# Causal masks moved from TensorE to VectorE and GpSimd in a decoder's self-attention, with the value products directly behind the shifts

## What is computed

```python
q = (x @ wq.T + bq).reshape(B, S, 16, 64).transpose(0, 2, 1, 3)     # likewise k and v
q, k = rope(q, k)
scores = einsum('bhqd,bhkd->bhqk', q, k)
scores = where(triu(ones((S, S)), k=1), -inf, scores)                # the causal mask
attn = softmax(scores / 8, axis=-1)
out = einsum('bhqk,bhkd->bhqd', attn, v)
x = layernorm(x + out @ wo.T + bo)
```

## Time and profile before

| | us |
|---|---|
| median of 3 runs | 2767.6 |
| lowest and highest | 2765.4 and 2783.56 |
| the profiled execution, its own time | 2774.03 |
| its span, first to last instruction | 2772.2 |
| mean granted TensorE clock | 0.896 |

### The profile page before, as it was taken

How to read it: one execution, slowest core, us unless ns; L and a number is a source line. 1 busy time by engine, 2 the same in 40 slices (tenths; PEclk the granted TensorE clock), 3 DMA queues, 4 the chain that set the end, 5 groups by cost and what they waited for, 6 DMA issues and landing times. The chain is left out here.

```text
span 2772.2 us, 46887 instructions
## 1 busy us (share of the span) xinstructions
PE 2118.1 (76%) x18469; PEld 1188.9 (43%) x18469; DVE 1536.0 (55%) x2539; ACT 1026.4 (37%) x1420; POOL 1026.9 (37%) x658
## 2 busy tenths in 40 slices
PE   6888888888888888888888886378586686783565
PEld 3434434434434444444444343256455464562222
DVE  4553553553644554544545531357767677677778
ACT  1322222232322222222222222058186293591555
POOL 0344344344434443443434444306326145053003
PEclk7999999999999999999999998699899798996685
DMA  6111111111112112112111100100000000001001
GB/s 185 24 29 41 28 44 41 28 29 41 28 37 49 28 22 48 28 22 47 26 25 35 30 20 5 52 6 3 6 2 2 6 3 2 7 3 33 0 0 61
DMA packets 51198, 78.02 MB, mean 28 GB/s; under 512 B 26144, under 2 KB 38560, under 8 KB 46112
## 3 DMA queue, kind: packets, MB, share of 16 engines
q1 hardware_dynamic: 41760, 74.71, 10.7%
q10 hardware_dynamic: 9216, 0.27, 0.2%
HBM read 36.68 MB, written 4.19 MB: 15 GB/s over the span
## 5 line engine op out<-in xcount | busy, mean ns | idle before, releaser
L639 POOL TENSOR_TENSOR acc<-acc,probs 128x1024 f32<-128x1024 f32 (+3 forms) x320 | 558.4, 1745 | 500.6 <-ACT probs L468 257.8
L468 ACT ACTIVATE probs<-psum 128x1024 f32<-128x1024 f32 (+3 forms) x384 | 292.2, 809 | 589.5 <-PE psum L364 335.4
L276 PE MATMUL psum<-xT,wqk 128*128 128x512 f32 x512 | 301.7, 746 | 94.7 <-ACT probs L468 52.0
L553 DVE TENSOR_REDUCE maxa<-psum 128x2 f32<-128x1024 f32 (+3 forms) x256 | 256.7, 1021 | 203.8 <-PE psum L327 139.3
L951 ACT ACTIVATE onehot<-psum 128x1024 bf16<-128x1024 f32 x320 | 323.0, 1038 | 14.9 <-DVE ctx L1101 8.3
L532 DVE TENSOR_TENSOR turned<-raw,rot 128x512 f32<-128x512 f32 x128 | 115.8, 905 | 379.9 <-ACT raw L451 350.8
L1246 POOL TENSOR_TENSOR vs<-vs,wgt 128x1280 f32 x64 | 151.7, 2371 | 444.7 <-DVE wgt L1093 444.7
L350 PE MATMUL psum<-operands 64*128 64x512 f32 (+3 forms) x1536 | 308.1, 517 | 10.1 <-ACT probs L468 5.1
L378 PE MATMUL psum<-probs,vals 128*64 128x512 f32 (+3 forms) x1536 | 290.1, 499 | 0.0
L850 PEld LDWEIGHTS psum<-piece,onehot 128*128 128x128 bf16 x7680 | 259.1, 99 | 71.5 <-ACT vs L955 14.2
L850 PE MATMUL psum<-piece,onehot 128*128 128x64 bf16 x7680 | 267.2, 194 | 9.2 <-ACT onehot L951 5.7
(11 more groups left out here) (194 smaller groups left out, 3003.0 us busy)
## 6 DMA issues: line engine op xcount, KB each, us to landing
operands<-turned SPq DMA_DIRECT2D x128, 256.0 KB, 4.1
wqk<-in_wqk SPq DMA_DIRECT2D x16, 512.0 KB, 3.0
xT<-in_xT SPq DMA_DIRECT2D x4, 1024.0 KB, 6.9
wv<-in_wv SPq DMA_DIRECT2D x16, 256.0 KB, 2.5
y<-in_x SPq DMA_DIRECT2D x1, 4096.0 KB, 21.7
wo<-in_wo SPq DMA_DIRECT2D x16, 256.0 KB, 2.6
out<-res SPq DMA_DIRECT2D x16, 256.0 KB, 2.1
bv<-in_bv SPq DMA_DIRECT2D x16, 128.0 KB, 3.2
```

Source lines behind the costliest of these rows:

```text
L276: last = nc.tensor.matmul(dst[:, eo, :], wqk[:, kt, c:c + P], x[:, kt, hf * BANK:(hf + 1) * BANK], start=kt == 0, stop=kt == KT - 1)
L468: nc.scalar.activation(probs[u % PBUF][:, :, 0:width], slot("s", n, u)[:, :, 0:width], ACT.Exp, scale=1.0 / D ** 0.5).then_inc(s_exp, 1)
L553: V.reduce_max(dst, slot("max", n, c)[:, :, 0:width], AX.X).then_inc(s_mread, 1)
L639: G.tensor_tensor(dst, dst, src, ALU.add).then_inc(s_acc, 1)
```

## The change

- `mask_q`, `mask_k`, `halves` and their matmuls go. A new fp32 tile `later` (0, and -1e30 above the diagonal) is loaded; three DMAs of constants become one.
- `maximum` on VectorE: for each of the 8 masked chunks one `tensor_tensor` adds `later` to the last 128 columns of both heads, in PSUM, then a wait for it, then the reduction.
- `add_probs` on GpSimd: for each of the 8 diagonal units one `affine_select` zeroes the probabilities above the diagonal in the first 128 columns of both heads in `probs`, counted by the new semaphore `s_tri`, then a wait for it, then the copy or addition.
- `weigh` on TensorE waits for `s_tri` where the unit is diagonal.
- `weigh` of units 2m-2 and 2m-1 stands directly behind the shifts of step m, ahead of the chunks and the full work. At m = 0 it stays where it was.

```diff
+DIAGONAL = [u for u, (kt, hf) in enumerate(UNITS_S) if kt * P >= hf * BANK]
+MASKED = [c for c, (qt, hf) in enumerate(CHUNKS) if (qt + 1) * P <= (hf + 1) * BANK]
...
-        halves = sb("halves", [P, 2, P], BF16)
-        mask_q = sb("mask_q", [P, 2, P], BF16)
-        mask_k = sb("mask_k", [P, 2, P], BF16)
+        later = sb("later", [P, P])
...
@@ max_chunk
                 for hh, rows in enumerate(HEADS):
                     last = nc.tensor.matmul(dst[:, hh, 0:width], ops[p][rows, 0, qt * P:(qt + 1) * P],
-                                            ops[p][rows, 1, hf * BANK:hf * BANK + width],
-                                            start=True, stop=not diag)
-                if diag:
-                    for part, cols in enumerate((slice(width - P, width), slice(width - D, width))):
-                        for hh, rows in enumerate(HEADS):
-                            last = nc.tensor.matmul(dst[:, hh, cols], halves[rows, part, :],
-                                                    mask_q[rows, part, D * part:P],
-                                                    start=False, stop=part == 1)
+                                            ops[p][rows, 1, hf * BANK:hf * BANK + width], start=True, stop=True)
@@ shift
                 for hh, rows in enumerate(HEADS):
                     last = nc.tensor.matmul(dst[:, hh, 0:width], first[rows, :], bias[n % 2][rows, a:a + width],
-                                            start=False, stop=not diag)
-                if diag:
-                    for part, cols in enumerate((slice(0, D), slice(0, P))):
-                        for hh, rows in enumerate(HEADS):
-                            last = nc.tensor.matmul(dst[:, hh, cols], halves[rows, part, :], mask_k[rows, part, cols],
-                                                    start=False, stop=part == 1)
+                                            start=False, stop=True)
@@ weigh
                 pe.wait_ge(s_exp, NU * n + u + 1)
+                if u in DIAGONAL:
+                    pe.wait_ge(s_tri, len(DIAGONAL) * n + DIAGONAL.index(u) + 1)
@@ the order of a step on TensorE
                     shift(n, 2 * m)
                     shift(n, 2 * m + 1)
+                    if m:
+                        weigh(n, 2 * m - 2)
+                        weigh(n, 2 * m - 1)
                     if n + 1 < PAIRS:
                         for c in CHUNKS_AT[m]:
                             max_chunk(n + 1, c)
...
-                    if m:
-                        weigh(n, 2 * m - 2)
-                        weigh(n, 2 * m - 1)
                     if m == 1 and n:
                         sums(n - 1)
@@ maximum
-                V.reduce_max(dst, slot("max", n, c)[:, :, 0:width], AX.X).then_inc(s_mread, 1)
+                if c in MASKED:
+                    corner = src[:, :, width - P:width]
+                    V.tensor_tensor(corner, corner, later[:, :].unsqueeze(1).broadcast_to([P, 2, P]), ALU.add)\
+                     .then_inc(s_mmask, 1)
+                    dve.wait_ge(s_mmask, len(MASKED) * n + MASKED.index(c) + 1)
+                V.reduce_max(dst, src[:, :, 0:width], AX.X).then_inc(s_mread, 1)
@@ add_probs
+                if u in DIAGONAL:
+                    block = probs[u % PBUF][:, :, 0:P]
+                    G.affine_select(block, block, [[0, 2], [1, P]], ALU.is_ge, 0.0, base=0, channel_multiplier=-1)\
+                     .then_inc(s_tri, 1)
+                    pool.wait_ge(s_tri, len(DIAGONAL) * n + DIAGONAL.index(u) + 1)
                 if kt == 0:
                     G.tensor_copy(dst, src).then_inc(s_acc, 1)
```

More of the change, by code:

```diff
@@ L135, in attention @@
         s_m = sem("max_scores")
+        s_mmask = sem("max_chunks_masked")
         s_mread = sem("max_chunks_reduced")
@@ L142, in attention @@
         s_exp = sem("probs_ready")
+        s_tri = sem("probs_masked")
         s_pv = sem("pv_done")
@@ L220, in _ @@
             load_v_weights(0)
-            for dst, src in ((rot, "rot"), (ident, "ident"), (halves, "halves"), (mask_q, "mask_q"), (mask_k, "mask_k")):
+            for dst, src in ((rot, "rot"), (ident, "ident"), (later, "later")):
                 sp.dma_start(dst[:], dram[src]).then_inc(s_const, 16)
@@ L318, in max_chunk @@
                 width = min(BANK, (qt + 1) * P - hf * BANK)
-                diag = (qt + 1) * P <= (hf + 1) * BANK
                 for hh, rows in enumerate(HEADS):
                     last = nc.tensor.matmul(dst[:, hh, 0:width], ops[p][rows, 0, qt * P:(qt + 1) * P],
-                                            ops[p][rows, 1, hf * BANK:hf * BANK + width],
-                                            start=True, stop=not diag)
-                if diag:
-                    for part, cols in enumerate((slice(width - P, width), slice(width - D, width))):
-                        for hh, rows in enumerate(HEADS):
-                            last = nc.tensor.matmul(dst[:, hh, cols], halves[rows, part, :],
-                                                    mask_q[rows, part, D * part:P],
-                                                    start=False, stop=part == 1)
+                                            ops[p][rows, 1, hf * BANK:hf * BANK + width], start=True, stop=True)
                 last.then_inc(s_m, 1)
@@ L356, in shift @@
                 kt, hf, a, width = span(u)
-                diag = kt * P >= hf * BANK
                 for hh, rows in enumerate(HEADS):
                     last = nc.tensor.matmul(dst[:, hh, 0:width], first[rows, :], bias[n % 2][rows, a:a + width],
-                                            start=False, stop=not diag)
-                if diag:
-                    for part, cols in enumerate((slice(0, D), slice(0, P))):
-                        for hh, rows in enumerate(HEADS):
-                            last = nc.tensor.matmul(dst[:, hh, cols], halves[rows, part, :], mask_k[rows, part, cols],
-                                                    start=False, stop=part == 1)
+                                            start=False, stop=True)
                 last.then_inc(s_s, 1)
@@ L397, in _ @@
                 project_v(0, u)
-            pe.wait_ge(s_const, 16 * 6)
+            pe.wait_ge(s_const, 16 * 4)
             pe.wait_ge(s_set, 5)
@@ L551, in maximum @@
                 dve.wait_ge(s_m, NCH * n + c + 1)
+                src = slot("max", n, c)
                 dst = maxb[:, :, qt - TT // 2] if hf else maxa[:, :, qt]
-                V.reduce_max(dst, slot("max", n, c)[:, :, 0:width], AX.X).then_inc(s_mread, 1)
+                if c in MASKED:
[4 more added lines that the diff above has]
+                V.reduce_max(dst, src[:, :, 0:width], AX.X).then_inc(s_mread, 1)
             def negate(n):
@@ L584, in residual @@
                  .then_inc(s_res, 1)
-            dve.wait_ge(s_const, 16 * 6)
+            dve.wait_ge(s_const, 16 * 4)
             dve.wait_ge(s_set, 5)
@@ L1735, in lay_attention @@
     o["ident"] = np.eye(128).astype(bf)
-    def halves(m):
-        return c(np.tile(m.reshape(2, 64, 128).transpose(1, 0, 2), (2, 1, 1)).astype(bf))
-    o["halves"] = halves(np.eye(128))
-    o["mask_q"] = halves(np.where(i[None, :] > i[:, None], -1e30, 0))
-    o["mask_k"] = halves(np.where(i[:, None] > i[None, :], -1e30, 0))
+    o["later"] = np.where(i[None, :] > i[:, None], -1e30, 0).astype(np.float32)
     o["rot"] = rope_tables()
```

## The result

The changed kernel takes 2965.8 us (median of 4 runs, 2960.1 to 2969.5) against 2775.6 for the kernel before in the same comparison: 1.067 times, 95% interval 1.065 to 1.070. The profiled execution's span went from 2772.2 to 2967.6 us, +195.4.

A forecast was written before the change was run, and what follows sets the result against it. TensorE (426 of 500 us busy) looked like the bound, but GpSimd's gaps around the broadcasts decide: odd +7.5, even +2.1, fifteen groups +144, with the ends +147 on 2774.0, 2921; 2912 for a median, range 2840 to 2990.

The forecast's parts named there:

- Reading GpSimd's gaps as occupied time that the select would stand behind: GpSimd around the broadcasts: about 5.9 us in and 7 back; weigh(9) waits some 9 us odd, 4 even.
- The odd pair: First exponential to unit 6's 24.4, to weigh(9) 25.4, to next pair 7.2: 57.0 us against 49.5, +7.5.
- The stretch behind `weigh(9)`: From weigh(9) to the next pair's first exponential: 7.2 us, bounds 5.6 and 9.5.
- The collision of the small combination with an addition: VectorE's 2.36 us combination beside a GpSimd addition, behind weigh(9): partly there; without it 2.2 us less.
- the 1.1 us allowed for it: Behind weigh(9): TensorE, idle for 4 to 9 us, starts at the lower clock, up to 1.1 us more.
- The even pair: Same three stretches, 24.7 + 26.6 + 7.2 = 58.5 us against 56.4, +2.1.
- Select 8 itself can slip in ahead of the gap or behind it; the sum is the same: GpSimd between broadcasts and addition 8: select 8's place leaves the time to weigh(9) unchanged, 25.4 odd, 26.6 even.
- the slack I gave VectorE and TensorE between unit 6 and `weigh(9)`: Between unit 6's exponential and weigh(9): about 9 us of slack in the odd pair, for TensorE, VectorE and ScalarE.
- Pair 0: The first pair, with no broadcast: gains 3 us.
- slow selects: Rival: GpSimd selects of 2.6 us each, 6.3 us a pair, +190 more, 3100 us; chance 0.10.
- a select that needs a change of its own: Rival: select runs from other code than the addition, each change pays 13 us, 256 times, 6100 us; chance 0.03.
- The rival on the other side: Rival: gap between broadcasts and addition 8 shrinks, weigh(9) is free; odd 48.5, even 52.6, in all 2690; chance 0.08.

The follow-up runs named there:

- move_only: The kernel before with only weigh moved directly behind the shifts, all masks still on TensorE: 2767.7 us, 0.995.
- select_only: The kernel before with only the diagonal units' masks moved to GpSimd selects, weigh in its old place, chunk masks on TensorE: 2937.1 us, 1.058.
- vector_only: The kernel before with only the chunks' masks moved to VectorE additions, units' masks still on TensorE: 2790.7 us, 1.005.
- after_no_adds: The changed kernel without VectorE's eight mask additions a pair, maxima taken over unmasked chunks: 2938.1 us, 1.057.
- dma_odd: The kernel before with reciprocal sums spread by DMA and weigh moved behind the shifts in odd pairs only, masks on TensorE: 2626.4 us, 0.944.
- after_same_code: The changed kernel with GpSimd's two partition_broadcast replaced by memsets, result not normalised: 2767.5 us, 0.995.
- before_same_code: The kernel before with GpSimd's two partition_broadcast replaced by memsets, result not normalised: 2659.7 us, 0.957.
- before_dma: The kernel before with the reciprocal sums spread over partitions by DMA through DRAM instead of GpSimd broadcasts, whole computation done: 2655.1 us, 0.958.
- dma_mixed: As before_dma, with weigh moved directly behind the shifts everywhere but in step 2 of the even pairs: 2659.2 us, 0.959.
- after_units_pe: The changed kernel with the diagonal units' masks back on TensorE and no selects; VectorE's additions and moved weigh stay: 2825.9 us, 1.016.

## Why the prediction came out as it did

The measured 2965.8 lies in the range of 2840 to 2990 and 54 us above the figure of 2912. By its steps:

- *Reading GpSimd's gaps as occupied time that the select would stand behind*: right. The wait is where it was put, up to 9.0 us, and about 8 and 4 us in the two pairs shown (48 waits in all; 31 were forecast, one a pair, so some of the 48 are other, short ones). The exponential's wait for GpSimd's addition went with it.
- *The odd pair*: 24.4 + 25.4 + 7.2 = 57.0 was forecast. Measured 734.74 - 710.25 = 24.5, then 25.0 to `weigh(9)` at 759.70, then 7.8: 57.25. The select was 0.46 and not 0.6 us, and it could run ahead of the gap. By the Trainium skill (GPSIMD Engine Reference, section Performance pitfalls for Q7 kernels) it would be an estimated 0.2 to 0.4 us, by its section Performance versus the Vector engine an estimated 2.6 us with data-dependent branching. The measured 0.46 lies near the first and excludes the second.
- *The stretch behind `weigh(9)`*: 7.2 was taken from between 5.6 and 9.5; 7.8 was measured in both pairs shown, and the medians are 7.1 in the odd and 7.5 in the even pairs. TensorE's share of it ran near the lower clock (0.60): the scores of units 0 and 1 took 3.19 us instead of 1.77. The collision of the small combination with an addition, which was in the sum for part of its 2.2 us, is here an operation of 0.60 us (2.36 before), while the clock took more than the 1.1 us allowed for it (1.4 in these scores alone): 7.2 came out right with two terms that made up for each other, which was luck.
- *The even pair* is where the sum was too small: 24.7 + 26.6 + 7.2 = 58.5 forecast; 25.7 + 27.9 + 7.8 = 61.4 in the pair shown, and 25.7, 27.5 and 7.5 in the medians (24.7 should have been 24.9 by its own terms: 28.7 - 1.2 - 2.6). Over pairs 1 to 30 the loss is 176 us (1740.9 us from the first exponential of pair 1 to that of pair 31, against 1564.7 before), where 144 was forecast: 107 in the odd pairs, 112 forecast, and 69 in the even ones, 32 forecast. Two sentences failed. "Select 8 itself can slip in ahead of the gap or behind it; the sum is the same" holds only while its exponential is early. Here it came at 809.77, select 8 idled 2.48 us, and the change back, which stands behind select 8 in GpSimd's order, began that much later. And the slack I gave VectorE and TensorE between unit 6 and `weigh(9)` I worked out for the odd pair only. In the even pair VectorE had none: the projection waited 5.48 us for it where it was 2.35 before.
- *Pair 0* was forecast to gain 3 us and lost 11.3 (51.8 to 63.1): with no broadcasts in its way nothing was thought to hold it, but it has the late VectorE too: its last projection waited 5.33 us for VectorE (2.25 before) and the scores of its last step 4.03 (move_only 64.3, select_only 51.4). That 14 and the 32 of the even and odd pairs together make 46 of the 48 us by which the profiled execution (2969.4) lies above its figure of 2921. The figure of 2912 for a median is 3 us too low by its own sum (2921 - 6.4 = 2915).
- *Why VectorE was later*: not its additions by themselves (vector_only +11 us, after_no_adds 28 us of 190), but the move. It takes TensorE sooner from a projection to the next scores, so that GpSimd's additions of units 6 and 7 begin while VectorE is still rotating; two operations are then stretched by 2 us each instead of one (794.89 and 797.55 against 820.91 and 821.52). I had counted the move as gain only. move_only shows the stretched pair without any of the other edits, dma_odd the gain where there is no rotation.
- *The rivals*: slow selects and a select that needs a change of its own are excluded (0.46 us, no gap between select and addition). The rival on the other side named what would have to go, the gap, and with it gone the changed kernel is level with before (2767). I had put 2690 to it: the odd pair is 46.0 instead of 48.5, but the even one 59.8 instead of 52.6.
- The share of each cause isn't one number. Taking away the selects gives 140 us back, the gaps 198, the additions 28; they overlap. Both causes are shown, each by runs without the other: the select behind the gap (select_only, +158 with `weigh` in its old place and no additions on VectorE) and VectorE's lateness in the even pairs (after_same_code against before_same_code, +108 with no gap). Which of them is the larger depends on which is taken away first.

## What to carry to other kernels

An engine's idle time that nothing in the profile ends is to be read as occupied until shown otherwise: before putting work on such an engine, ask what stands in its order on either side of that time, and who will wait for it. Work that was only a by-product (sums that nobody waits for soon) can stand behind a stall; work on the way to the next matmul cannot. And where pairs of iterations differ, the slack has to be worked out for each kind; a reordering that gains in one can bring two engines together in the other.

## What the runs showed of the hardware

- GpSimd's change between copies or additions and `partition_broadcast` takes 5.9 to 6.1 us in and 6.7 to 7.2 us back in the rows shown, in the mean of the changed kernel 6.0 (184.5/31) and 7.1 (220.7/31). It goes with the broadcasts alone: without them, in before_same_code and before_dma, it is not there. The packed traces name what begins it, in records that the views leave out: two MODIFY_POOL_CONFIG of GpSimd, 0.04 us apart, at the start of each change, into the broadcast (773.44 and 773.48 before the broadcast at 779.18) and back (781.78 and 781.81 before the addition at 788.82). In its self-attention the kernel before has 130 of them, two for each of its 64 changes and two at the start; before_dma, dma_mixed, dma_odd and both kernels with memsets have only the two at the start there. What GpSimd does behind such a record until it works again no run shows. The Trainium skill (GPSIMD Engine Reference, section Instruction dispatch) has about 6 us for the first call to freshly loaded code; the way back is longer here. `affine_select` ran on either side without a change of its own and without such a record.
- VectorE and GpSimd hold each other up: operations of VectorE with both inputs in SBUF take 2.7 to 2.8 us instead of 0.69 beside GpSimd additions of 2.4 us (less where only part of them lies beside one), two additions of GpSimd beside them 5.53 us instead of 4.86, and an `affine_select` 0.86 instead of 0.41. Reductions from PSUM keep their 1.2 us and additions to PSUM their 0.42. The Trainium skill (GPSIMD Engine Reference, section Key points) names VectorE instructions with two SBUF inputs as those that contend; the runs agree.
- After waits of 2.4 to 5.5 us the next projection ran 5.4 to 6.4 us instead of 3.70 in the rows shown, at a granted clock of 0.57 where it ran 6.43. The length of the wait alone doesn't decide it: in dma_mixed 14 projections behind a wait of 1.9 us ran 3.70 us, in after_units_pe four behind 1.6 to 1.9 us ran 5.3 to 5.4.
